# A 64-step gated feed-forward kernel with per-sequence LoRA: a plain first step, and one transfer instead of two for each gathered LoRA block

## The reference, cut to what matters

```
# x: (64 sequences, 64 tokens, 512); adapter index a[b] in 0..7 for each sequence b; rank 16; I = 2048
gate = x @ Wg + (x @ Ag[a]) @ Bg[a]
up   = x @ Wu + (x @ Au[a]) @ Bu[a]
h    = silu(gate) * up
x1   = x + h @ Wd + (h @ Ad[a]) @ Bd[a]
y    = x1 + x1 mixed over the 64 tokens of each sequence by weights[a]   # einsum 'bct,bcd->bdt'
```

## Time and profile before

| | us |
|---|---|
| Median of 3 runs | 1218.6 (1215.49 to 1220.42) |
| The profiled execution's own time | 1219.65 |
| Its span in the trace | 1218.0 |
| PE busy in it | 1163.6 |
| DVE busy in it | 913.6 |
| Mean granted clock of TensorE, share of full | 0.982 |

### The profile page before, as it was taken

How to read it: one execution, slowest core, us unless ns; L and a number is a source line. 1 busy time by engine, 2 the same in 40 slices (tenths; PEclk the granted TensorE clock), 3 DMA queues, 4 the chain that set the end, 5 groups by cost and what they waited for, 6 DMA issues and landing times.

```text
span 1218.0 us, 23035 instructions
## 1 busy us (share of the span) xinstructions
PE 1163.6 (96%) x6720; PEld 1034.8 (85%) x6720; DVE 913.6 (75%) x1578; ACT 539.3 (44%) x902; POOL 256.3 (21%) x405
## 2 busy tenths in 40 slices
PE   4889999999999997999999999998899999999998
PEld 3678888887888886888888788887899999999997
DVE  6776777876787787678887788888667766776775
ACT  4544444543444443344453344456344444444442
POOL 5223221112201012220101111011322221231230
PEclk8899999999999999899999999999999999999999
DMA  5597876688667589666759978868777777667781
GB/s 188 161 308 241 244 222 180 170 235 262 189 180 234 171 238 264 190 194 187 233 166 274 280 223 252 243 215 307 244 265 244 244 239 273 232 230 274 231 277 66
DMA packets 155583, 276.26 MB, mean 227 GB/s; under 512 B 28898, under 2 KB 97634, under 8 KB 155330
## 3 DMA queue, kind: packets, MB, share of 16 engines
q1 hardware_dynamic: 133104, 213.48, 57.5%
q0 software_dynamic: 21488, 59.66, 14.6%
q10 hardware_dynamic: 866, 1.66, 0.4%
HBM read 200.23 MB, written 74.45 MB: 226 GB/s over the span
## 4 chain that ended last, share of the span: by engine, by line
PE 73%; SPq 9%; DVE 5%; DMA 5%; issue 4%; ACT 3%; POOL 1%; POOLq 0%; DVEq 0%; ACTq 0%
PE ps L1368 12%; PE ps L1369 12%; PE ps L1370 12%; PE ps L1517 8%; PE ps L1519 8%; PE ps L1518 8%; PE ps L1380 7%; SPq L276 7%; DMA bq<-b_dram 2%; PE ps L1398 2%; DMA h_raw<-h_dram 1%; DMA xst<-xg 1%; SPq L245 1%; ACT xo_hi L602 1%; SPq L199 1%
## 5 line engine op out<-in xcount | busy, mean ns | idle before, releaser
L1368 PE MATMUL ps<-xo_hi,w_hi 128*128 128x512 f32 x896 | 359.3, 401 | 12.0 <-DVE w_lo L886 10.7
L1369 PE MATMUL ps<-xo_lo,w_hi 128*128 128x512 f32 x896 | 354.8, 396 | 0.0
L1370 PE MATMUL ps<-xo_hi,w_lo 128*128 128x512 f32 x896 | 351.8, 393 | 0.0
L1368 PEld LDWEIGHTS ps<-xo_hi,w_hi 128*128 128x128 f32 x896 | 171.4, 191 | 43.0 <-DVE w_lo L886 10.7
L1370 PEld LDWEIGHTS ps<-xo_hi,w_lo 128*128 128x128 f32 x896 | 170.4, 190 | 38.2
L473 POOL DMA_DIRECT2D h_dram<-hs x128 | 96.0, 754 | 487.3 <-DVE hs L1001 247.9
L886 DVE TENSOR_TENSOR hl<-h_raw,hh 128x1024 fp32r<-128x1024 f32 x112 | 137.0, 1223 | 79.0 <-ACT hh L602 77.6
L1380 PEld LDWEIGHTS ps<-t_st,bq 128*128 128x128 f32 x1024 | 158.5, 193 | 44.2 <-DMA bq<-b_dram 18.0
L1369 PEld LDWEIGHTS ps<-xo_lo,w_hi 128*128 128x128 f32 x896 | 171.1, 191 | 26.6
L1380 PE MATMUL ps<-t_st,bq 128*128 128x256 f32 x1024 | 166.2, 286 | 21.7 <-DMA bq<-b_dram 15.9
L602 ACT ACTIVATE hh<-h_raw 128x1024 fp32r<-128x1024 f32 x112 | 117.9, 1053 | 113.3 <-DMA h_raw<-h_dram 72.0
(11 more groups left out here) (153 smaller groups left out, 2188.0 us busy)
## 6 DMA issues: line engine op xcount, KB each, us to landing
bq<-b_dram SPq DMA_DIRECT2D x992, 64.0 KB, 2.6
h_raw<-h_dram SPq DMA_DIRECT2D x112, 512.0 KB, 5.3
h_dram<-hs POOLq DMA_DIRECT2D x128, 256.0 KB, 4.2
raw<-packed SPq DMA_DIRECT2D x58, 512.0 KB, 4.0
h_dram<-h_f SPq DMA_DIRECT2D x96, 256.0 KB, 3.9
ad_raw<-a_d SPq DMA_DIRECT2D x64, 128.0 KB, 2.1
xs<-x POOLq DMA_DIRECT2D x16, 512.0 KB, 5.8
y_out_dram<-xs POOLq DMA_DIRECT2D x30, 256.0 KB, 4.7
```

Of the source, the lines that this page charges most:

```text
L1368: pe.matmul(bank, st[0], mv[0], start=start and kk == 0, stop=False, skip_group_check=True)
L1369: pe.matmul(bank, st[0], mv[1], start=False, stop=False, skip_group_check=True)
L1370: m = pe.matmul(bank, st[1], mv[0], start=False, stop=kk == 1, skip_group_check=True)
```

## The change

It has two parts. **The first step** is done without Strassen's scheme: eight plain products of the four quarters of W with B11, B21, B12, B22 (`plain`), each of which waits for high and low parts separately; its results are copied and not summed (`keep_c11_first` and others). The sums T1, T2, T3, NT4 are made by VectorE meanwhile, for step 1, and the first product of step 1 stands among the LoRA products of step 0 (`first_product`). `a_all` goes; A of each sequence is fetched by a transfer of 64 KB that GpSimd issues, and put in order by ScalarE (first group) or GpSimd (`order_a`). `bq0_lo` moves from GpSimd to VectorE. In GpSimd's list b_lo, store_b and load_b move behind the stores of h. **The LoRA rows** are in another order: row r of sequence s (of four) is r * 4 + s in each half, so that one transfer with a repeated source fills both halves, 32 partitions with step 4.

```diff
-GATHER = SLOTS * 2 * 16
+GATHER = SLOTS * 16
-X_ORDER = [(B11, B21, T1, T2, T3, B22, NT4)] + [XOPS] * (GROUPS - 1)
+X_ORDER = [(B11, B21, B22, T1, T2, T3, NT4)] + [XOPS] * (GROUPS - 1)
...
                 for b in range(first, last):
-                    for half in range(2):
-                        r = half * QR + (b % QS) * RANK
-                        sp.dma_start(bq[n % 2][r:r + RANK, b // QS, :, :].bitcast(F32).rearrange("r k c -> r (k c)"),
-                                     b_dram[piece_of(g, k), bass.ds(slot_numbers[g * SLOTS + b], 1)].rearrange("a r c -> (a r) c"))\
-                            .then_inc(bq_in[n % 4], 16)
+                    sp.dma_start(bq[n % 2][b % QS:P:QS, b // QS, :, :].bitcast(F32).rearrange("r k c -> r (k c)"),
+                                 b_dram[piece_of(g, k), bass.ds(slot_numbers[g * SLOTS + b], 1)].to_broadcast([2, RANK, PIECE * BC]))\
+                        .then_inc(bq_in[n % 4], 16)
...
                 for s in range(QS):
                     a = number(pool, g * SLOTS + q * QS + s)
-                    pool.tensor_copy(aq[q if g == 0 else 0][:, :, s, :], a_all[:, bass.ds(a, 1), :, :].rearrange("p a k r -> p (a k) r"))\
-                        .then_inc(a_gathered, 1)
+                    pool.dma_start(a_raw[0 if g else q + 1][:, s, :, :].rearrange("p k r -> p (k r)"),
+                                   a_gu[bass.ds(a, 1)].rearrange("a p c -> (a p) c")).then_inc(a_in[q], 16)
+
+            def order_a(g, q):
+                pool.wait_ge(a_in[q], 16 * QS * (g + 1))
+                pool.wait_ge(t_done, g * QUADS + q)
+                pool.tensor_copy(aq[0][:, :, :, :], a_raw[0][:, :, :, :].rearrange("p s k r -> p k r s")).then_inc(a_ordered, 1)
...
             load_b(0)
-            pool.wait_ge(x_in[B12], 16)
-            pool.wait_ge(x_in[B22], 16)
-            pool.tensor_tensor(xst[T3][:, :], xst[B22][:, :], xst[B12][:, :], ALU.subtract).then_inc(t3_first, 1)
+            pool.wait_ge(idx_in, 16)
+            for q in range(QUADS):
+                gather_a(0, q)
             b_lo(0)
             store_b(0)
...
             x_first(B11)
-            w_lo_raw(0)
+            w_lo_first(0)
+            w_lo_first(1)
             x_first(B21)
-            for k in range(4):
-                w_add(0, k)
+            w_lo_first(2)
+            x_lo_b12()
+            x_first(B22)
             x_add(0, 1, None)
-            w_lo_sum(0, 0)
             x_add(0, 2, None)
-            x_first(T1)
-            x_first(T2)
-            w_lo_sum(0, 1)
...
             for k in range(4):
                 w_add(1, k)
             w_lo_raw(1)
+            x_first(T1)
+            bq0_lo(0)
+            dve.wait_ge(const_in, 48)
+            t_mask(0, 0)
+            x_first(T2)
+            t_lo(0, 0)
+            w_lo_sum(1, 0)
+            t_mask(0, 1)
+            x_add(0, 0, None)
+            t_lo(0, 1)
             t_mask(0, 2)
-            make_u3(0)
             t_lo(0, 2)
-            w_lo_sum(1, 0)
+            x_first(T3)
             t_mask(0, 3)
+            bq0_lo(1)
             t_lo(0, 3)
+            keep_c11_first()
             w_lo_sum(1, 1)
...
             def step_0():
+                a11, a12, a22, a21 = range(4)
+                plain(RB[0], a11, 0, True, x_hi_done, x_lo_done, 1, 1).then_inc(p1_done, 1)
+                plain(RB[0], a12, 3, False, x_hi_done, x_lo_done, 2, 2).then_inc(p5_done, 1)
+                plain(RA[0], a22, 3, True, x_hi_done, x_lo_done, 2, 2).then_inc(p6_done, 1)
+                plain(RA[0], a21, 0, False, x_hi_done, x_lo_done, 1, 3)
                 lora_a(0, 0)
+                plain(RC[0], a11, 6, True, b12_hi_done, b12_lo_done, 1, 1)
+                plain(RD, a21, 6, True, b12_hi_done, b12_lo_done, 1, 3).then_inc(p7_done, 1)
                 lora_a(0, 1)
+                plain(RC[0], a12, 5, False, x_hi_done, x_lo_done, 3, 2)
                 lora_a(0, 2)
+                plain(RD, a22, 5, False, x_hi_done, x_lo_done, 3, 2)
                 lora_a(0, 3)
                 pe.wait_ge(bq0_lo_done, 1)
                 pe.wait_ge(t_lo_done, 4)
                 lora(RB[0], 0, 0, 0, False).then_inc(p2_done, 1)
                 lora(RA[0], 0, 1, 0, False).then_inc(p4_done, 1)
+                first_product(1)
...
-        "slot_mask": (np.arange(P)[:, None] % QR // RANK == np.arange(QS)[None, :]).astype(np.float32),
+        "slot_mask": (np.arange(P)[:, None] % QS == np.arange(QS)[None, :]).astype(np.float32),
```

More of the change, by code:

```diff
@@ L142, in cond_resid_kernel @@
         b_dram = nc.dram_tensor("b_dram", (PIECES, ADAPTERS, RANK, PIECE * BC), F32, kind="Internal").ap()
-        idx_in, a_in, const_in = sem("idx_in"), sem("a_in"), sem("const_in")
+        idx_in, const_in = sem("idx_in"), sem("const_in")
+        a_in = [sem(f"a_in{q}") for q in range(QUADS)]
         x_in = [sem(f"x_in{k}") for k in range(4)]
@@ L559, in _ @@
                 late = LATE_T if g == 0 else 0
[L560 to L564, removed]
                 if g + 1 < GROUPS and 4 <= c - late < 8:
-                    gather_a(g + 1, c - late - 4)
+                    order_a(g + 1, c - late - 4)
+                if g + 1 < GROUPS and 3 <= c - late < 7:
+                    gather_a(g + 1, c - late - 3)
                 if s == 2 * CH:
@@ L607, in x_hi @@
                     act.wait_ge(x_in[src], 16 * (g + 1))
-                elif g == 0 and src == T3:
-                    act.wait_ge(t3_first, 1)
-                else:
-                    act.wait_ge(x_added[src], g if src == T3 else g + 1)
+                else:
+                    act.wait_ge(x_added[src], g + 1)
+                if g == 0 and src == NT4:
+                    act.wait_ge(p7_done, 1)
                 if g:
@@ L926, in w_lo_raw, with w_lo_first, x_lo_b12, bq0_lo @@
                 lo(w_lo[s % 2][:, 0:3 * WB], raw[s % 2][:, 0:3 * WB], w_hi[s % 2][:, 0:3 * WB]).then_inc(w_lo_done, 1)
+            def w_lo_first(part):
+                dve.wait_ge(w_hi_done, part + 1)
+                cols = (slice(0, WB), slice(WB, 3 * WB), slice(3 * WB, 4 * WB))[part]
+                lo(w_lo[0][:, cols], raw[0][:, cols], w_hi[0][:, cols]).then_inc(w_lo_done, 1)
+            def x_lo_b12():
+                dve.wait_ge(b12_hi_done, 1)
+                lo(xo_lo[6][:, :], xst[B12][:, :], xo_hi[6][:, :]).then_inc(b12_lo_done, 1)
+            def bq0_lo(pair):
+                q = slice(2 * pair, 2 * pair + 2)
+                dve.wait_ge(bq0_hi_done, pair + 1)
+                lo(bq[0][:, q, :, WB:2 * WB], bq_raw[:, q, :, :], bq[0][:, q, :, 0:WB]).then_inc(bq0_lo_done, 1)
+            def keep_c11_first():
+                dve.wait_ge(p2_done, 1)
+                dve.tensor_copy(p1_s[:, :], RB[0]).then_inc(c11_done, 1)
+            def keep_c22_first():
+                dve.wait_ge(l22_done, 1)
+                dve.tensor_copy(v22[:, :], RD).then_inc(v22_done, 1)
+            def keep_c12_first():
+                dve.wait_ge(p3_done, 1)
+                dve.tensor_copy(u2_s[:, :], RC[0]).then_inc(c12_done, 1)
             def w_lo_sum(s, half):
@@ new lines, in plain @@
+            def plain(bank, w, k, start, x_hi_sem, x_lo_sem, x_count, w_count):
+                wc = [slice(w * WB + kk * P, w * WB + (kk + 1) * P) for kk in range(2)]
+                xc = [slice(kk * HALF, (kk + 1) * HALF) for kk in range(2)]
+                pe.wait_ge(w_hi_done, w_count)
+                pe.wait_ge(x_hi_sem, x_count)
+                for kk in range(2):
+                    pe.matmul(bank, w_hi[0][:, wc[kk]], xo_hi[k][:, xc[kk]], start=start and kk == 0, stop=False,
+                              skip_group_check=True)
+                pe.wait_ge(x_lo_sem, x_count)
+                for kk in range(2):
+                    pe.matmul(bank, w_hi[0][:, wc[kk]], xo_lo[k][:, xc[kk]], start=False, stop=False, skip_group_check=True)
+                pe.wait_ge(w_lo_done, w_count)
+                for kk in range(2):
+                    m = pe.matmul(bank, w_lo[0][:, wc[kk]], xo_hi[k][:, xc[kk]], start=False, stop=kk == 1,
+                                  skip_group_check=True)
+                return m
@@ L1492, in step @@
                 lora(RC[par], s, 0, 1, False).then_inc(p3_done, 1)
[L1494 removed]
+                pe.wait_ge(u3_done, s)
+                if s == 1:
+                    ready(NT4)
                 if new:
```

218 lines of the change are left out of this document (105 added, 113 removed).

## The result

The changed kernel takes 1987.8 us (median of four runs, 1985.6 to 1989.1) where the kernel before takes 1218.7: a ratio of 1.631, interval 1.628 to 1.635. The forecast of two DMA engines came in, 4% quicker than its 2080.

A forecast was written before the change was run, and what follows sets the result against it. PE, busy 1163.6 of 1218.0 us, was taken to bound the kernel before. With gathers on two engines, 1285 + 380 gives a 1665 us stage; 26 + 1665 + 23 + 396 = 2110, taken as 2080; range 1183 to 2450.

The forecast's parts named there:

- forecast A: Merged gathers of B: outermost count 2 confines each to two DMA engines; 2080 us, own range 1850 to 2800, chance 0.65.
- the bounds 2 and 16: Merged gathers of B: DMA engines that an outermost count of 2 could give, 16 meaning no change; 2 was taken.
- the rate of an engine: Gathers of B: 32.5 MB on each of two DMA engines at 25.3 GB/s, giving 1285 us.
- the 580: First stage: 0.75 of 774 us, each engine's sixteenth of all traffic; less the gathers' 155 to 241, leaves 380 us.
- The slower bound of 16.3 GB/s: Gathers of B: an engine's rate where little but gathers is in flight, giving 1994 us instead of 1285.
- some 30 times by 20 us and more: Sign of two engines: PE's waits for `bq`, once each pair of steps.
- about 0.35: Sign of two engines: mean DMA share of the first stage, down from 0.75.
- land near 67: Start: the first gathered piece, 2.1 MB over two engines in 41 us, lands near 67 us.
- rival B: Merged gathers: shape does not confine them, issue halves at no price; 1195 us, 1183 to 1208, chance 0.22.
- The first step: Start: first matmul near 9 us, step 1 ends near 48.5 instead of 60.2; 11.7 us won, ends 5 and 14.
- ScalarE's four reorderings lie beside DVE's longer list: Start, first group's A: four reorderings on ScalarE at 0.6 us each, costed at nothing.
- cost at nothing: A loads: 64 of 64 KB issued by GpSimd at 0.52 us each, covered by its idle time, no cost counted.

The follow-up runs named there:

- experiment 2: Changed kernel, each gather reading 32 rows in a row from a DRAM table stored twice, first piece in two transfers a sequence: 1229.0 us, ratio 1.010.
- experiment 3: As experiment 2, but the two copies of 16 rows stand one row apart in DRAM, a source of two blocks: 1999.6 us.
- experiment 4: As experiment 3, but 4 blocks of 8 rows, one row apart, stored by 16 small transfers for each piece: 1431.4 us.
- experiment 5: As experiment 4, but 8 blocks of 4 rows, one row apart: 1251.3 us.
- experiment 6: The change's first step and A loads alone, with old LoRA row order and two gathers into contiguous partitions: 1208.0 us, ratio 0.993 to the kernel before.
- experiment 7: As experiment 2, but the first piece also comes from a doubled input, in 16 transfers: 1218.1 us, ratio 1.002 to the kernel before.

## Why the prediction was right, point by point

**Two engines (forecast A): right.** Experiments 2 and 3 keep the count of transfers, the bytes and the partitions: 32 rows merged 1229, two blocks 2000. Experiments 4 and 5 and the closing packets make the number of engines the cause. The choice of 2 between the bounds 2 and 16 held. The page of the Trainium skill that was weighed there, "DMA: Bandwidth & Descriptors", says that the count is the largest number up to 16 that divides the slowest dimension above 1 of both patterns. The order of 2, 4, 8 and merged rows agrees with it, and so does the real step in experiment 3: its "Rules for kernel authors" speak of any outermost dimension under 16, of which the broadcast is their example.

**The size: the term that was mis-sized is the rate of an engine.** I took 25.3 GB/s and so 1285 us for the gathers, and 380 us for the rest on the same engines. From the first gather at 33.4 us to the last, issued at 1545.3, plus its landing, are some 1530 us. If the two engines are full all that time, then with G for the gathers and O for all else G + O = 1530, and the mean over 16 engines is G/8 + O = 0.34 x 1537 = 523. That gives G = 1151 and O = 379: the rest was right, and an engine moves 32.5 MB in 1151 us, 28.2 GB/s. The 134 us of difference in the gathers are more than the 122 between 2110 and the measured time, and the 30 us taken off for overlap were too few. What makes the rate 11% higher, overlap or something else, no run separates. The split itself is an estimate: it takes the two engines' share as exactly 1, and shares up to 1.09 occur in the earlier trace rows. Free of it is the sum of bytes: 114 GB/s over these 1530 us, the rest of it spread evenly, is some 39 MB on each of the two engines, 25.7 GB/s. That the rest met 380 is partly luck: 380 takes the gathers out of the 580 at some 20 GB/s. At the 25.3 that the gathers' own term uses it is 425, and the sum 2155. With four engines the same numbers give 1151/2 + 379 = 954 us for the stage and, with the 458 around it, 1412; experiment 4 measured 1431. With eight they give 667, less than the 775 that PE needs, and experiment 5 is at 1251. The slower bound of 16.3 GB/s was far off.

**Signs in the trace.** Waits for `bq` "some 30 times by 20 us and more": 31, mean 23.2. Share "about 0.35": 0.34. `raw` and `h_dram` late: 17.5 and 14.7 us. Second stage "keeps its 396 us": 402.5. The first gathered piece was to "land near 67": too early. Its gathers started at 33.4 and not at 26, the last was issued at 33.45 + 32.79 = 66.2 us, and PE's wait for the piece ended at 82.11 us:

```profile
82.11 1.22 PE L1421 MATMUL ps<-t_st,bq 128*128 128x256 f32 x4 [20.67 <-DMA bq<-b_dram]
```

**"The issue would halve at no price" (rival B): wrong.** The step put 0.49 us on a gather whatever its shape. Measured on SP, median: 0.367 us for 16 partitions in a row, 0.537 for 16 that lie 4 apart, 0.472 for 32 that lie 4 apart. One gather for two costs 0.47 instead of 0.73, two thirds and not half. And with plain rows it needs a table stored twice, whose 35 us eat the 14 to 25 that it gains. B's 1195 was not to be had in the ways tried; experiments 2 and 7 give 1229 and 1218.

**The first step: right in direction, short of its size.** First matmul "near 9": 9.01. Step 1 was to end near 48.5, against 60.2 before. In experiment 6 it ends at 51.43. The shortfall is not in the waits: the sum had 4 us for those, and they came to 0.54 and 2.92, the longer at 47.85 us for DVE's `v` of step 1. It is in what the sum left out. The last LoRA product of step 0 was released at 34.29 and not at 33, and behind the longer wait the matmuls run at 0.43 us again, some 1.7 us until 51.43. (The sum as written, 33.2 + 10.7 + 4, is 47.9 and not 48.5.) Won are 8.7 us there and 10 in the whole (1208.0 against 1217.8); the range of 5 to 14 held. These are the PE rows of experiment 6, last LoRA product of step 0, the wait, and the end of step 1:

```profile
34.29 1.18 PE L1425 MATMUL ps<-t_st,bq 128*128 128x256 f32 x8 [2.37 <-DVE t_st L902]
...
47.85 0.80 PE L1413 MATMUL ps<-xo_hi,w_hi 128*128 128x512 f32 x1 [2.92 <-DVE v L1004]
...
50.58 1.05 PE L1425 MATMUL ps<-t_st,bq 128*128 128x256 f32 x4
51.43 0.63 PE L1413 MATMUL ps<-xo_hi,w_hi 128*128 128x512 f32 x1
```

**"ScalarE's four reorderings lie beside DVE's longer list": right alone, wrong in the changed kernel.** There PE waits 6.5 us for A at 30.23 us: ScalarE's order puts the rounding of the first B ahead of the last two reorderings, and that B comes over two engines until 25.5. A reordering also takes 1.09 to 1.16 us there, not 0.6, with the rows in the new order; in experiment 6, in the old order, it takes 0.62 to 0.63. The last LoRA product of step 0 starts at 41.43 instead of 34.29. In experiment 6 PE's wait for A is 0.47 us. The A loads, "cost at nothing", are not quite free: ScalarE waits 3.15 us for the second four of them, until 17.79, on the chain that leads to the end of step 1.

## What to carry to other kernels

Look at the outermost count of a transfer's pattern before merging two transfers into one: a leading 2 left two of 16 DMA engines. Its signs in a profile were a mean DMA share of a third with everything waiting, and fewer packets for the same bytes. If the DMA engines look idle and loads are late all the same, divide the bytes by the time: here a working engine moved an estimated 26 to 28 GB/s. An issue has a price that depends on the partitions it writes; where one queue issues a thousand of them, measure that price before a layout is chosen.

## What the runs showed of the hardware that I had not expected

- SP's time for one transfer depends on the destination: 0.367 us for 16 contiguous partitions, 0.537 for 16 at a step of 4 (992 transfers each, the same source), 106 us over the kernel, while the landing stayed at 2.5 to 2.7 us.
- A real step of two blocks costs as much as a repeat (1999.6 against 1987.8 us).
- Storing the table twice, 4 MB more, cost 35 us, most of it before 200 us, where the DMA share was 0.80 to 0.88. Whether the bytes did it or the new form of the stores (outermost count 8, landing in 8.9 us for 3.8), and what they hold up, was not separated.
- The reordering of A on ScalarE takes 1.09 to 1.16 us with the rows of four sequences interleaved, and 0.62 to 0.63 with each sequence's rows together.
